# A fifth slot for queries and keys, its load placed behind the store of the maxima

## The chip, the cores and the metric

One core of one Trainium2 chip runs the whole program. The metric is the device time of one execution in microseconds (us). PE is the matrix engine (TensorE), DVE the vector engine, ACT the scalar engine, POOL GpSimd, SP the engine that only issues transfers here. "SPq" in a row is SP's queue of issues.

## The reference

A gated cross-attention block followed by a quantised feed-forward block, for x of 16 x 100 x 512 and a context of 16 x 361 x 512:

```python
Q = (layernorm(x) @ Wq) / sqrt(32)        # 16 heads of 32, in 4 groups
K, V = ctx @ Wk, ctx @ Wv                 # 4 heads of 32
scores = Q K^T + slope[h] * (key - query) # alibi, then the mask
x = x + tanh(g0) * (softmax(scores) V) @ Wo
q = round(layernorm(x), 8 bits per row);  Wg, Wu, Wd = ternary weights
h = rms_norm(silu(q Wg) * (q Wu)) * ln_w
x = x + tanh(g1) * round(h, 8 bits per row) @ Wd
```

A ternary weight is clip(round(w / mean|w|), -1, 1), so the mean over a whole weight must be known before the first one can be quantised.

## The kernel before

Everything is float32 in the attention. There are four stages.

1. **Queries** (to about 60 us). x is normalised, turned and projected in groups of four batches; each query tile is split into a high and a low float32r half and stored to `q_scratch` in DRAM.
2. **Context** (to about 148 us). For each of 16 batches `ct` is loaded, values go to `v_all`, keys (high and low) to `k_all`, which lies over the space that `w_q` takes later.
3. **Attention** (about 150 to 330 us). A batch needs its queries and keys in a *slot*: `qs[slot]` and `ks[slot]`, 103 rows, that `load_qk(b)` (line 397) gathers by six transfers on SP's queue: two from `q_scratch` (L402, 400 and 200 KB), three from `k_all` (L404, 181 KB each), and one of the mask row (L409). 1143 KB in all. Rows 96 to 102 hold constants (the alibi terms), written once for each slot. There are four slots; batch b uses slot b % 4. Slots 0 to 2 have their own space and get their constants from DVE; the fourth, `qs_late` and `ks_late`, lies over the context tiles, so that it exists only when the context stage is done; POOL copies its constants from slot 0 (`late_rows`, line 518).
4. **Feed-forward** (about 330 us to the end), in 13 tiles of rows.

In the attention PE works in *steps*, one per batch, of eight units each. In step b it computes the scores of batch b (`scores`, L1355, two matmuls per unit, whose row maxima DVE takes at L1021), and between them, by the table `BEHIND`, the transposed scores of older batches (`scores_t`, L1369), whose exponentials ACT takes at L725, and the products with values and ones (L1381, L1384). `scores_t(b - 1, 0)` is in unit 5 of step b; `scores_t(b - 2, 11)`, the last that reads slot (b - 2) % 4, stands in the same unit ahead of it.

The transposed scores need the maxima of their batch as two more rows (101 and 102) of the slot. DVE splits the maxima at the end of a step (`split_max`, L1028 and L1030), PE turns them in unit 1 of the next (L1392), ACT copies them to `nm_t`, and SP stores them into the slot with two transfers of 6.2 KB (`store_max`, L394). `scores_t(b, 0)` waits for both (`nm_in`). ACT waits for them too before it overwrites `nm_t` a step later.

SP issues strictly in this order, in `attention_step(b)` (line 424): `store_max(b - 1)`, then a wait until `scores_t(b - 2, 11)` is done, then `load_qk(b + 2)`. For b = 1 it is `store_max(0)`, a wait for the last key, the loads of batch 3, `store_max(1)`, a wait for POOL's constants, the mask row.

Meanwhile POOL quantises the feed-forward weights (`quantise`, line 532): 24 pieces of 128 x 1024, each a load of 512 KB on POOL's own queue and three operations (L535, L537, L542). The last writes `w_q`, over `k_all`, so piece n waits until the batches whose keys lie there are in their slots (L541). At the end of the attention PE waits for all 24. In step 9 ACT makes `wo_h` from `wo_f`, in step 10 DVE makes `wo_l` (L1079).

## Time and profile before

| | us |
|---|---|
| median of three runs | 527.29 |
| the three runs | 515.03, 527.29, 527.6 |
| the profiled execution | 515.34 |
| its span, first to last instruction | 513.5 |
| PE busy in the span | 466.4 (91%) |
| DVE / ACT / POOL busy | 368.2 / 320.5 / 230.5 |

The profiled execution stands with the lowest of the three runs; two of the three are about 12 us above it. All durations below are of the profiled one. Idle time in square brackets behind a row is that of the engine just before it, with what ended it.

### The profile page before, as it was taken

Reading aid. Unit: us, or ns where it says so; the run is one execution under the profiler, and the core shown is the slowest. Engines: PE = TensorE matmul, PEld = TensorE weight load, DVE = VectorE, ACT = ScalarE, POOL = GpSimd, SP = SyncE. Lnnn points to the kernel's source line nnn. Section 1 sums busy time; section 2 is a strip of 40 time slices with the busy share of each in tenths; the row PEclk is TensorE's granted clock in tenths of the full one; section 3 lists DMA queues with packets and bytes.
Section 4 is the critical chain, followed back from the end, with each engine's and each line's share of the span. In section 5 each row is a group of like instructions: output and inputs, shape, how many; then the busy total and the mean of one; then the engine's idle time right before and its main releaser. Section 6 shows DMA issues by size and latency. Waiting matters only on the chain.

```text
span 513.5 us, 8312 instructions
## 1 busy us (share of the span) xinstructions
PE 466.4 (91%) x2854; PEld 299.2 (58%) x2854; DVE 368.2 (72%) x674; ACT 320.5 (62%) x560; POOL 230.5 (45%) x250
## 2 busy tenths in 40 slices
PE   0699989999899999998899998988999999999966
PEld 0699989989875454554445554444444545555522
DVE  4778554448667887888978894377777778777762
ACT  0366626755656656666666666577777777777760
POOL 1100000000126787776362681057777777777630
PEclk9999998999999999999999999999999999999988
DMA  7879888899968889899676813014434333333323
GB/s 189 252 226 399 293 300 315 245 331 252 280 153 182 197 185 246 210 221 228 137 159 152 217 43 104 1 31 107 100 93 93 77 88 91 89 86 93 71 52 72
DMA packets 62834, 85.51 MB, mean 167 GB/s; under 512 B 37362, under 2 KB 48834, under 8 KB 61006
## 3 DMA queue, kind: packets, MB, share of 16 engines
q1 hardware_dynamic: 57614, 59.87, 47.3%
q0 software_dynamic: 3456, 12.58, 8.4%
q10 hardware_dynamic: 1728, 12.58, 7.0%
q8 instruction: 21, 0.34, 0.3%
q14 instruction: 15, 0.12, 0.1%
HBM read 57.94 MB, written 9.85 MB: 132 GB/s over the span
## 4 chain that ended last, share of the span: by engine, by line
PE 50%; DVE 15%; ACT 12%; DMA 12%; issue 6%; SPq 2%; ACTq 0%; POOL 0%; DVEq 0%; POOLq 0%
PE wide L1459 8%; DMA ct<-ctx_t 7%; PE bank L1288 6%; PE wide L1288 6%; PE bank L1381 5%; PE bank L1369 5%; PE bank L1329 5%; PE wide L1355 5%; PE bank L1469 5%; PE bank L1384 5%; DVE row_max L1021 3%; DMA qs<-nm_t 3%; ACT p_t L725 2%; DMA wq_f<-wq 2%; ACT act L837 2%
## 5 line engine op out<-in xcount | busy, mean ns | idle before, releaser
L1021 DVE TENSOR_REDUCE row_max<-wide 100x2 f32<-100x722 f32 x128 | 109.9, 903 | 21.0 <-PE wide L1355 20.0
L725 ACT ACTIVATE p_t<-bank 121x400 f32<-121x400 f32 x192 | 91.5, 506 | 52.5 <-PE bank L1369 49.3
L1459 PE MATMUL wide<-w_q,xq 128*128 128x512 bf16 x384 | 86.9, 380 | 2.7 <-DVE h L1139 2.4
L576 POOL TENSOR_TENSOR z<-h,lnw 128x512 f32<-128x512 f32 x48 | 61.1, 1275 | 15.2 <-DVE h L1139 14.6
L1459 PEld LDWEIGHTS wide<-w_q,xq 128*128 128x128 bf16 x384 | 35.5, 98 | 51.6 <-DVE h L1139 8.0
L1369 PE MATMUL bank<-qs,ks 103*121 103x400 f32 x144 | 52.0, 390 | 8.1 <-ACT p_t L725 5.5
L530 POOL DMA_DIRECT2D quant_in<-w_ffn x24 | 14.3, 597 | 98.0 <-PE bank L1329 91.5
L1329 PE MATMUL bank<-wv_f,ct 128*121 128x128 f32 x384 | 46.3, 278 | 4.0 <-DMA ct<-ctx_t 4.0
L968 DVE TENSOR_TENSOR ctl<-ct,cth 128x1445 fp32r<-128x1445 f32 x16 | 26.6, 1664 | 31.3 <-ACT cth L635 31.3
L1469 PE MATMUL bank<-w_q,yq 128*128 128x512 bf16 x192 | 46.5, 396 | 1.8 <-DMA yq<-y_int 1.7
L1329 PEld LDWEIGHTS bank<-wv_f,ct 128*121 128x121 f32 x384 | 45.4, 189 | 4.6 <-DMA ct<-ctx_t 4.6
L855 ACT ACTIVATE z<-z,small 128x1024 f32<-128x1024 f32 x24 | 29.7, 1237 | 29.5 <-DVE small L1173 29.5
L1369 PEld LDWEIGHTS bank<-qs,ks 103*121 103x121 f32 x144 | 25.3, 183 | 38.8 <-ACT p_t L725 15.5
L1355 PE MATMUL wide<-ks,qs 101*100 101x362 f32 x192 | 44.1, 333 | 2.1 <-ACT nm_t L635 1.5
L1139 DVE TENSOR_TENSOR h<-act,wide 128x512 f32<-128x512 f32 x50 | 34.2, 686 | 13.8 <-ACT act L837 13.5
L1381 PE MATMUL bank<-p_t,v_all 120*32 120x400 f32 (+1 forms) x384 | 42.9, 519 | 0.0
L1384 PE MATMUL bank<-p_t,ones_keys 120*32 120x400 f32 (+1 forms) x384 | 41.2, 501 | 0.0
L542 POOL TENSOR_SCALAR w_q<-quant_in 128x1024 bf16<-128x1024 f32 x24 | 27.5, 1147 | 25.2 <-DMA ks<-m_scratch 20.9
L837 ACT ACTIVATE act<-wide,small 128x512 f32<-128x512 f32 x50 | 33.7, 677 | 7.4 <-PE wide L1459 7.2
L535 POOL TENSOR_SCALAR quant_in<-quant_in,small 128x1024 f32<-128x1024 f32 x24 | 27.5, 1147 | 17.4 <-DMA quant_in<-w_ffn 16.6
L1469 PEld LDWEIGHTS bank<-w_q,yq 128*128 128x128 bf16 x192 | 19.0, 101 | 27.2 <-DMA yq<-y_int 3.9
L1355 PEld LDWEIGHTS wide<-ks,qs 101*100 101x100 f32 x192 | 30.5, 166 | 6.5 <-DVE row_max L1021 3.1
(160 smaller groups left out, 920.5 us busy)
## 6 DMA issues: line engine op xcount, KB each, us to landing
quant_in<-w_ffn POOLq DMA_DIRECT2D x24, 512.0 KB, 6.4
ct<-ctx_t SPq DMA_DIRECT2D x16, 722.0 KB, 10.6
abs_b<-w_ffn ACTq DMA_DIRECT2D x7, 1024.0 KB, 10.1
ks<-k_all SPq DMA_DIRECT2D x36, 181.0 KB
q_scratch<-qhl SPq DMA_DIRECT2D x16, 400.0 KB, 5.9
abs_a<-w_ffn ACTq DMA_DIRECT2D x5, 1024.0 KB, 6.6
qs<-q_scratch SPq DMA_DIRECT2D x12, 400.0 KB
xb<-x SPq DMA_DIRECT2D x12, 256.0 KB, 2.9
```

The source lines that it names most:

```text
L576: nc.gpsimd.tensor_tensor(z[par][0:rows, c], h[0:rows, c], lnw[0:rows, c], ALU.mult).then_inc(z_done, 1)
L725: nc.scalar.activation(p_t[:, j, :], bank[j % 2][0:KT, 0:HQ], ACT.Exp).then_inc(exp_done, 1)
L837: nc.scalar.activation(silu_g[j % 2][0:rows, :], wide[j % 2][0:rows, 0, :], ACT.Silu, scale=f_cg[par][0:rows]).then_inc(silu_done, 1)
L1021: nc.vector.tensor_reduce(row_max[b % 2][:, 2 * u:2 * u + 2], wide[u % 2][0:SQ, :, 0:SK], AX_X, ALU.max).then_inc(s_maxed, 1)
L1288: mm = nc.tensor.matmul(dst, a, b, start=(n == 0), stop=(n == last))
L1329: mm = nc.tensor.matmul(bank[2 + b % 2][0:KT, kt * P:(kt + 1) * P], tile[:, c * SK + k0:c * SK + k0 + KT], wv_f[:, c, :], start=(c == 0), ...
L1355: mm = nc.tensor.matmul(wide[u % 2][0:SQ, k, 0:SKP], qs[b % SLOTS][0:ROWS_S, g, h * SQ:(h + 1) * SQ], ks[b % SLOTS][0:ROWS_S, g, :], start ...
L1369: nc.tensor.matmul(bank[j % 2][0:KT, 0:HQ], ks[b % SLOTS][:, g, KT_AT[kt]:KT_AT[kt] + KT], qs[b % SLOTS][:, g, :], start=True, stop=True). ...
L1381: nc.tensor.matmul(bank[2][32 * g:32 * g + 32, 0:HQ], v_all[0:n, b, kt * P + DH * g:kt * P + DH * (g + 1)], p_t[0:n, kt * G + g, :], start ...
L1384: mm = nc.tensor.matmul(bank[3][32 * g:32 * g + 32, 0:HQ], ones_keys[0:n, :], p_t[0:n, kt * G + g, :], start=(kt == 0), stop=(kt == 2), ti ...
L1459: mm = nc.tensor.matmul(wide[j % 2][0:rows, m, :], xq[par][:, c, 0:rows], w_q[:, m * C + c, 512 * j:512 * j + 512], start=(c == 0), stop=( ...
L1469: mm = nc.tensor.matmul(bank[1][0:rows, :], yq[:, k, 0:rows], w_q[:, 2 * C + k // 4, (k % 4) * D:(k % 4 + 1) * D], start=(k == 0), stop=(k ...
```

## The change

There are five slots; batch b uses slot b % 5. The queries of both late slots and the keys of the fourth lie over the context tiles; the keys of the fifth lie at the end of the memory, where `log_sum` was, and `log_sum` moves over the context tiles. SP fills the constants of slots 3 and 4 by four transfers out of slot 0, and POOL's copies go. SP's order becomes `store_max(b - 1)`, a wait until `scores_t(b - 3, 11)` is done, `load_qk(b + 2)`. `wo_l` is written over `wo_f`. `oh` and `ol` move over the dead values of the first batches, and other feed-forward tiles move by some KB. Slot 0 is now read by the last batch, and the first product of the feed-forward (`h`, which lies over slot 0) waits for its transposed scores.

```diff
-SLOTS = 4
-LATE_SLOT = 3
+SLOTS = 5
+EARLY_SLOTS = 3
@@ memory
+    (qs3, ks3, qs4, log_sum), r_wo = over(r_c, ("qs3", [ROWS, G, HQ], F32R), ("ks3", [ROWS, G, SKP], F32R),
+                                          ("qs4", [ROWS, G, HQ], F32R), ("log_sum", [P, HQ], F32))
...
-    log_sum = new("log_sum", [P, HQ], F32)
+    ks.append(new("ks4", [ROWS, G, SKP], F32R))
...
-    (wo_f, wo_h, wo_l), e = over(
-        r_wo, ("wo_f", [P, HPG, D], F32), ("wo_h", [P, HPG, D], F32R), ("wo_l", [P, HPG, D], F32R))
+    (wo_l, wo_h), e = over(r_wo, ("wo_l", [P, HPG, D], F32R), ("wo_h", [P, HPG, D], F32R))
-    (oh, ol), e = over(r_wo, ("oh", [P, HPG, P], F32R), ("ol", [P, HPG, P], F32R))
+    (wo_f,), e = over(r_wo, ("wo_f", [P, HPG, D], F32))
@@ SP
+            def late_rows():
+
+                for slot in range(EARLY_SLOTS, SLOTS):
+                    for rows, src in ((qs[slot][96:101, :, :], qs[0][96:101, :, :]), (ks[slot][96:103, :, :], ks[0][96:103, :, :])):
+                        sp.dma_start(rows.bitcast(F32), src.bitcast(F32)).then_inc(rows_in, 16)
...
-                if b == LATE_SLOT:
+                if b == EARLY_SLOTS:
                     store_max(1)
-                    sp.wait_ge(late_set, 2)
+                    sp.wait_ge(rows_in, 64)
...
             def attention_step(b):
+                if b != 2:
+                    store_max(b - 1)
                 if b == 1:
-                    store_max(0)
                     sp.wait_ge(kl_ready, B)
-                    load_qk(LATE_SLOT)
-                elif b > 2:
-                    store_max(b - 1)
-                if 2 <= b < B - 2:
-                    sp.wait_ge(st_done, (b - 1) * UNITS)
+                    late_rows()
+                if b >= 3:
+                    sp.wait_ge(st_done, (b - 2) * UNITS)
+                if b < B - 2:
                     load_qk(b + 2)
@@ POOL
-            def late_rows():
-
-                pool.wait_ge(kl_ready, B)
-                pool.wait_ge(nm_split, 4)
-                nc.gpsimd.tensor_copy(qs_late[96:101, :, :], qs[0][96:101, :, :]).then_inc(late_set, 1)
-                nc.gpsimd.tensor_copy(ks_late[96:103, :, :], ks[0][96:103, :, :]).then_inc(late_set, 1)
-                pool.wait_ge(late_set, 2)
...
-            late_rows()
@@ DVE, by_up
-                if j == 0 and not (isinstance(t, int) and t == 0):
+                if j == 0 and isinstance(t, int) and t == 0:
+                    dve.wait_ge(st_done, B * UNITS)
+                elif j == 0:
                     dve.wait_ge(z_done, t * NJ)
```

## Rows read from the trace of the kernel before

**Rows 1.** The page, its first part: busy time of each engine in the span.

```profile
PE 466.4 (91%) x2854; PEld 299.2 (58%) x2854; DVE 368.2 (72%) x674; ACT 320.5 (62%) x560; POOL 230.5 (45%) x250
```

**Rows 2.** Windows, one attention step each: length, busy us, granted clock, DMA share, GB/s.

```profile
152.02:162.62 10.60, 10.54 (x79) 5.71 (x77) 7.77 (x11) 6.28 (x16) 9.52 (x10) 1.00 0.82 181
...
196.06:207.69 11.63, 10.37 (x78) 5.71 (x77) 9.06 (x14) 7.12 (x19) 8.22 (x9) 1.00 1.02 239
...
229.73:240.96 11.23, 10.96 (x78) 5.76 (x78) 9.94 (x14) 7.19 (x18) 8.70 (x9) 1.00 0.90 222
240.96:253.19 12.23, 10.44 (x78) 5.78 (x78) 10.85 (x14) 8.66 (x19) 4.87 (x5) 1.00 0.73 170
253.19:266.68 13.49, 12.17 (x79) 6.27 (x77) 10.87 (x15) 7.35 (x19) 8.60 (x8) 0.87 0.62 138
266.68:277.24 10.56, 10.30 (x78) 5.72 (x77) 8.79 (x14) 7.12 (x19) 3.80 (x4) 1.00 0.73 167
...
sum 158.06, PE 148.87 PEld 80.09 DVE 134.52 ACT 101.68 POOL 104.41; mean PE 10.63 PEld 5.72 DVE 9.61 ACT 7.26 POOL 7.46
```

**Rows 3.** Timeline of PE and PEld in the attention: start, us, instruction, idle before.

```profile
158.35 0.29 PEld L1369 LDWEIGHTS bank<-qs,ks 103*121 103x121 f32 x2 [0.65 <-DMA qs<-nm_t]
...
169.94 0.63 PE L1369 MATMUL bank<-qs,ks 103*121 103x400 f32 x2 [0.96 <-DMA qs<-nm_t]
...
203.42 0.63 PE L1369 MATMUL bank<-qs,ks 103*121 103x400 f32 x2 [1.00 <-DMA qs<-nm_t]
...
283.84 0.63 PE L1369 MATMUL bank<-qs,ks 103*121 103x400 f32 x2 [0.23 <-DMA qs<-nm_t]
...
310.87 0.39 PE L1288 MATMUL wide<-wo_h,oh 128*128 128x512 f32 x1
```

**Rows 4.** Timeline of SP's queue: when transfers are issued, and for how long.

```profile
149.07 1.13 SPq L402 DMA_DIRECT2D qs_late<-q_scratch  x2
150.24 1.95 SPq L404 DMA_DIRECT2D ks_late<-k_all  x3
152.88 1.21 SPq L394 DMA_DIRECT2D qs<-nm_t  x2
...
156.97 1.13 SPq L402 DMA_DIRECT2D qs<-q_scratch  x2
...
163.59 1.22 SPq L394 DMA_DIRECT2D qs<-nm_t  x2
167.53 1.42 SPq L402 DMA_DIRECT2D qs<-q_scratch  x2
...
271.60 1.13 SPq L402 DMA_DIRECT2D qs<-q_scratch  x2
...
278.21 1.22 SPq L394 DMA_DIRECT2D qs<-nm_t  x2
```

**Rows 5.** The tile `nm_t`: time from issue to landing of its 24 stores into early slots.

```profile
DMA to landing us min/median/max: 1.7/3.6/10.9
```

**Rows 6.** Timeline of POOL: the copies, and a weight piece that waited, the first `ol`.

```profile
151.23 1.52 POOL L522 CAST qs_late<-qs 5x1600 fp32r<-5x1600 f32 x1 [13.79 <-DVE nm_q L1030]
...
154.22 1.12 POOL L535 TENSOR_SCALAR quant_in<-quant_in,small 128x1024 f32<-128x1024 f32 x1
...
283.56 1.05 POOL L542 TENSOR_SCALAR w_q<-quant_in 128x1024 bf16<-128x1024 f32 x1 [8.01 <-DMA ks<-m_scratch]
...
305.10 2.39 POOL L565 TENSOR_TENSOR ol<-o_t,oh 128x512 fp32r<-128x512 f32 x1
```

**Rows 7.** Timeline of DVE: the split of the maxima slow and quick, and `wo_l`.

```profile
239.19 1.50 DVE L1028 TENSOR_SCALAR nm_q<-row_max 100x16 fp32r<-100x16 f32 x1
...
251.75 0.18 DVE L1028 TENSOR_SCALAR nm_q<-row_max 100x16 fp32r<-100x16 f32 x1
...
252.05 2.28 DVE L1079 TENSOR_TENSOR wo_l<-wo_f,wo_h 128x2048 fp32r<-128x2048 f32 x1
```

**Rows 8.** Windows: the five microseconds in which the granted clock fell.

```profile
255.00:260.00 5.00, 4.79 (x25) 2.32 (x26) 4.02 (x6) 1.55 (x5) 2.53 (x3) 0.66 0.17 35
```

More of the change, by code:

```diff
@@ L138, in flamingo_block @@
     r_a = place[0]
-    (qs_late, ks_late), r_wo = over(r_c, ("qs_late", [ROWS, G, HQ], F32R), ("ks_late", [ROWS, G, SKP], F32R))
-    qs = [qs_late if i == LATE_SLOT else new(f"qs{i}", [ROWS, G, HQ], F32R) for i in range(SLOTS)]
-    ks = [ks_late if i == LATE_SLOT else new(f"ks{i}", [ROWS, G, SKP], F32R) for i in range(SLOTS)]
+    (qs3, ks3, qs4, log_sum), r_wo = over(r_c, ("qs3", [ROWS, G, HQ], F32R), ("ks3", [ROWS, G, SKP], F32R),
+                                          ("qs4", [ROWS, G, HQ], F32R), ("log_sum", [P, HQ], F32))
+    qs = [new(f"qs{i}", [ROWS, G, HQ], F32R) for i in range(EARLY_SLOTS)] + [qs3, qs4]
+    ks = [new(f"ks{i}", [ROWS, G, SKP], F32R) for i in range(EARLY_SLOTS)] + [ks3]
     r_p = place[0]
@@ L178, in flamingo_block @@
     assert e <= r_a
-    (wo_f, wo_h, wo_l), e = over(
-        r_wo, ("wo_f", [P, HPG, D], F32), ("wo_h", [P, HPG, D], F32R), ("wo_l", [P, HPG, D], F32R))
+    (wo_l, wo_h), e = over(r_wo, ("wo_l", [P, HPG, D], F32R), ("wo_h", [P, HPG, D], F32R))
     assert e <= r_i
-    (oh, ol), e = over(r_wo, ("oh", [P, HPG, P], F32R), ("ol", [P, HPG, P], F32R))
+    (wo_f,), e = over(r_wo, ("wo_f", [P, HPG, D], F32))
     (lnw,), e = over(r_i, ("lnw", [P, F], F32))
     assert e <= r_a
-    (xb0, xb1, x1_0, x1_1, xd, xq_f, xq0, xq1, x_int, act0, act1, ident_b), e = over(
-        r_v, ("xb0", [P, D], F32), ("xb1", [P, D], F32), ("x1_0", [P, D], F32), ("x1_1", [P, D], F32),
-        ("xd", [P, D], F32), ("xq_f", [P, D], F32), ("xq0", [P, C, P], BF16), ("xq1", [P, C, P], BF16), ("x_int", [P, D], BF16), ("act0", [P, 512], F32),
-        ("act1", [P, 512], F32), ("ident_b", [P, P], BF16))
+    (oh, ol, xb0, xb1, x1_0, x1_1, xd, xq_f, xq0, ident_b, act0, act1, xq1, x_int), e = over(
+        r_v, ("oh", [P, HPG, P], F32R), ("ol", [P, HPG, P], F32R), ("xb0", [P, D], F32), ("xb1", [P, D], F32),
+        ("x1_0", [P, D], F32), ("x1_1", [P, D], F32), ("xd", [P, D], F32), ("xq_f", [P, D], F32), ("xq0", [P, C, P], BF16),
+        ("ident_b", [P, P], BF16), ("act0", [P, 512], F32), ("act1", [P, 512], F32), ("xq1", [P, C, P], BF16), ("x_int", [P, D], BF16))
     assert e <= r_c
@@ L252, in flamingo_block @@
         alibi_set = sem("alibi_set")
-        late_set = sem("late_set")
+        rows_in = sem("rows_in")
         mask_set = sem("mask_set")
```

## The prediction

> **What bounds the kernel now.** I read the page first, then the chain that ended last, then PE's timeline through the attention, then SP's queue beside it. PE is busy 466.4 of 513.5 us [rows 1], so time can be won only where PE stands still. The change touches nothing ahead of 149 us and no work behind about 333 us, so the question is what PE loses in the 14 attention steps between.
>
> A table of windows cut at the turn of the maxima gives the steps: 158.06 us for 14. The two shortest are 10.60 and 10.56 us, with PE busy 10.54 and 10.30 [rows 2]: that is a step in which nothing is late. At 10.56 each, 14 steps would take 147.8, so 10.2 us is lost, and it goes to three causes.
> - Three steps hold a stop of PE at `scores_t(b, 0)` that a store of maxima ended: 0.96, 1.00 and 0.23 us, 2.2 in all [rows 3]. The step around the second is 11.63 long, 1.0 more than a free one [rows 2].
> - The steps in which `wo_h` and `wo_l` are made: 12.23 and 13.49 [rows 2], 4.6 us of loss. `wo_l` holds DVE for 2.28 us while maxima wait [rows 7], and behind it the granted clock is 0.66 over five microseconds, in part the lower of its two levels (1.2 instead of 2.4 GHz), after a step in which PE was busy only 10.44 of 12.23 us [rows 2, 8]. That alone is 5 x 0.34 = 1.7 us.
> - The rest, 10.2 - 2.2 - 4.6 = 3.4 us, lies in steps such as the one of 11.23 [rows 2], near whose end the split of the maxima took 1.50 us where it takes 0.18 otherwise [rows 7]; POOL was busy 8.70 us of it [rows 2].
>
> Why is a store late? SP's queue shows it. `store_max` is issued in unit 1 (163.59), and PE wants it in unit 5. The load of 1143 KB ahead of it was issued at 156.97 [rows 4]. In a step with such a stop the transfers' share is 1.02 [rows 2]: the engines are full, with POOL's weight loads among them. Late in the stage a wait of POOL dates the end of a load: the load begun at 271.60 landed just ahead of 283.56 (11.7 to 12.0 us), and POOL's piece had waited 8.01 us for it [rows 4, 6]. The store issued at 278.21 stood behind it and PE got it at 283.84 [rows 3, 4]. In the 11 steps without a stop on a store it was in time. So a store lands with the load ahead of it, and is late when that is over 5.4 us after its own issue (168.98 less 163.59, [rows 3, 4]). Its shortest landing is 1.7 us, the median 3.6 [rows 5].
>
> The Trainium skill, page "DMA: Bandwidth & Descriptors", section "Queues, rings and completion order", says that descriptors of one engine are taken in ring order and that a semaphore's increment lands only after every earlier write from that engine. By that rule a load put behind the store costs the store nothing; by the opposite case (both share the bandwidth) the store would take about its median and still be in time. The trace agrees with the rule: the store landed with the load ahead of it. The sum below does not need it.
>
> **The change, part by part.**
>
> *Load behind the store, steady state.* The load waits for a batch that finished a step ago, so it is issued 1.2 us after the store's issue began: 164.8 instead of 167.53, or 268.9 instead of 271.60 [rows 4], 2.7 us earlier. With 12.0 us to land, 268.9 gives 280.9, 2.7 us after the next store's issue at 278.21; PE needs the store 5.4 us after it. The stops of 1.00 and 0.23 us go: -1.2. Bounds: 0, if weight loads take the room that is freed; and -2.4, if the median landing hides small delays elsewhere; I take -1.2, the rows themselves. The fifth slot means that no load waits for PE and that no score waits for a load: none did before.
>
> *Late rows on SP.* This is the part with a price. From 149.07 SP issues four more transfers. An issue is 0.57 to 0.65 us (1.13 for two, 1.95 for three) [rows 4], so 4 x 0.6 = 2.4 us. Then come the five of the load, 3.1 us, so `store_max(1)` is issued at 154.6 and not at 152.88: 1.7 later, for 0.7 us of waiting for ACT was there to absorb it. PE wants it at 158.35; there the wait before was 0.65 us, its usual gap [rows 3]. The store needs between 3.6 us (median, [rows 5]) and 6.3 (163.59 to 169.9, [rows 3, 4]) from issue: it lands at 158.2 to 160.9, a stop of 0 to 2.5 us. Nearest is a store behind one uncontended load (that load began at 149 with an empty queue), so I take the lower middle, +1.0. The copies move 5 x 6400 and 7 x 5792 bytes per slot, 145 KB in all: at 181 GB/s [rows 2] 0.8 us of transfer, inside those bounds. If fewer transfer engines share them it is still under the 2.4 us of issue. `rows_in` is awaited after ten later issues, so it costs nothing; what is queued behind that wait is the mask row and the next load, whose reader starts at 161.5.
>
> *The second store.* The load of batch 4 now follows the mask row (one more issue of 0.6 behind the store's two) at about 156.4 instead of 156.97, only 0.5 us earlier, and behind a first load that began 2.4 us later. So `store_max(2)` still stands in a full queue. But PE comes to it 1.0 later by the part above. The stop of 0.96 us goes to about 0.1: -0.9 (bounds: 0 and -0.96).
>
> *POOL without copies.* POOL starts weight pieces at 151.4 and not at 154.22 [rows 6], 2.9 us sooner. Later pieces wait for loads that come 2.7 us sooner. The last operation then ends near 302 instead of 305; behind it stands `ol` (305.10) [rows 6], which is done at 307.5 and which PE takes only at 310.87, without a wait [rows 3]. Worth 0, hidden behind attention on PE; without that cover at most 2.9.
>
> *Contention.* The moved pieces meet other DVE operations. The 3.4 us of the third cause may vanish or double: 0, bounds -3.4 and +3.4. The Trainium skill, page "SBUF — State Buffer", section "Who interferes with whom", says that GpSimd and certain VectorE operations take one port pair as an exclusive lock, the later one blocking for a whole instruction. The slow splits beside a busy POOL agree. It gives no sign for this change.
>
> *`wo_l` in place.* Same instruction, same size: 0. The transfer of `wo_f` comes earlier with the load ahead of it, and ACT reads it steps later: 0. The clock's fall stays as long as `wo_l` blocks DVE: 0, bounds -1.7 (it does not fall) and +1.7 (it falls once more).
>
> *The added wait on DVE.* `by_up(0, 0)` needs the first silu, which ACT runs only after the last four exponentials of batch 15, and these follow the last transposed scores. The wait is over before it is reached: 0; behind it would stand all of DVE's feed-forward work. SP's waits in steps 14 to 16 are for batches done a step before: 0. Moved tiles change no instruction's size: 0.
>
> Sum: +1.0 - 0.9 - 1.2 = -1.1. Profiled execution 515.34, so **514.2 us**. Against the median shown, 527.29, that is 13 less, but 12 of these are the distance of the profiled execution from the median and not the change; a median from the upper cluster would be 527.3 - 1.1 = 526.2.
>
> **The rivals.**
> 1. *The start costs more than the stops give (slower).* `store_max(1)` lands at 160.9, and, because load 3, load 4 and the copies are now back to back in a full queue, `store_max(2)` is late by another 1.7 us. +2.5 + 1.7 - 1.2 = +3.0: 518.3. It decides from a landing of `store_max(1)` after about 159.8 us. For it: a share of 1.02 in the step at 196. Against it: step 2 has 0.82, so there was room. Chance 0.2.
> 2. *Late stores are the 12 us.* The upper runs are 12.0 to 12.3 us above the profiled one, and 14 steps with a stop of 0.87 us would be just that; the two long stops seen are 0.96 and 1.00. If transfers are a little slower there, the change takes all of it: about 514 in every run, 2.4% under the median. For it: the fit, and stores that land close to the need. Against: two such tight clusters look like no matter of transfer rates. Chance 0.14.
> 3. *Contention falls as well.* Stops and slow splits all go: 515.34 - 2.2 - 3.4 = 509.7. Chance 0.12.
> 4. *No effect.* Weight loads fill the room that the earlier load leaves, and the stops stay: 515 to 516. Chance 0.1.
>
> **How the numbers follow.** The forecast has the remaining 0.44. All but the second rival lie within 2% of before if like runs are compared (about what a measurement of this kernel can tell from no change); 2% is 10.3 us, more than all that the steps lose, so faster has 0.14 of the second rival and 0.02 of luck. Slower by 2% needs 0.7 us in every step: a contention that locks on, 0.06. The range runs from 509.5 (third rival) to 527 (the forecast in the upper cluster); the forecast's own is 511 to 517.
>
> **What would show it.** Right: no stop on `nm_t` at PE from step 4 on; loads on SP's queue 1.2 us behind the store's issue; POOL's waits for slots shorter by 2 to 3 us; a stop of about 1 us at `scores_t(1, 0)`; FFN unchanged from its first product on. Wrong: stops of PE by stores in later steps; a `store_max(1)` landing past 160; more than five slow splits at L1028; another fall of the clock.

## The result, and the profile after

| | before | after |
|---|---|---|
| median, us | 521.69 (12 executions) | 526.92 (12 executions) |
| lowest to highest | 515.03 to 529.72 | 524.45 to 531.14, and one of 927.18 |
| profiled execution | 515.34 | 525.0 |
| its span | 513.5 | 523.1 |
| mean granted clock in it | 0.987 | 0.972 |

The changed kernel takes 1.0131 times as long (95% interval 1.01 to 1.0162): 1.3% slower, where -1.1 us was forecast. This ratio leaves out the slow executions of each kernel (more than 1.5% above its fastest), which the medians in the table include; the medians alone are 1.0% apart. The execution of 927.18 us left no trace; its cause is open, and the median doesn't hang on it. The two profiled executions are 9.6 us of span apart, more than the 5.2 us between the medians, since the profiled one of before was among its quickest. Eight of the 12 executions of before lie between 519.7 and 523.9, where the first three had none: the prediction's "upper cluster" was an accident of three draws.

The page after, busy time of each engine and the line of the granted clock in 40 slices ([rows 1] before):

```profile
PE 469.3 (90%) x2854; PEld 301.4 (58%) x2854; DVE 365.7 (70%) x674; ACT 320.2 (61%) x560; POOL 225.8 (43%) x248
...
PEclk9999998999996999999789999999999999999998
```

The same number of matmuls is 2.9 us longer on PE, so only part of the 9.6 us is standing still; the clock line has a 6 and a 7 in the attention. Windows after, cut at the turn of the maxima as in [rows 2] (length, busy us of PE, PEld, DVE, ACT, POOL, granted clock, DMA share, GB/s):

```profile
151.28:171.42 20.14, 12.99 (x78) 6.70 (x77) 7.33 (x11) 6.26 (x16) 12.05 (x14) 0.75 0.94 189
...
182.53:193.09 10.56, 10.30 (x78) 5.71 (x77) 8.87 (x14) 7.12 (x19) 8.49 (x9) 1.00 0.94 207
...
246.59:261.83 15.24, 13.19 (x79) 7.16 (x77) 9.43 (x14) 9.12 (x20) 5.62 (x7) 0.78 0.56 127
261.83:275.76 13.93, 12.37 (x78) 6.10 (x77) 11.86 (x15) 7.23 (x19) 8.35 (x7) 0.88 0.70 162
275.76:286.32 10.56, 10.30 (x79) 5.70 (x77) 8.86 (x14) 7.11 (x19) 2.81 (x4) 1.00 0.69 163
```

Where the 9.6 us are:

| part | before | after | difference |
|---|---|---|---|
| up to the first turn | 152.02 | 151.28 | -0.7 |
| step 2 | 10.60 | 20.14 | +9.5 |
| the steps with `wo_h` and `wo_l` | 12.23 + 13.49 | 15.24 + 13.93 | +3.4 |
| the other eleven steps | 121.74 | 118.07 | -3.7 |
| from the last turn to the end | 203.42 | 204.44 | +1.0 |

One step lost as much as the whole kernel did; the other differences cancel out. PE's timeline after, the stops of its matmuls in the attention that are over 0.5 us ([rows 3] before):

```profile
164.76 1.02 PE L1367 MATMUL bank<-qs,ks 103*121 103x400 f32 x2 [7.10 <-DMA qs<-nm_t]
...
221.19 0.62 PE L1367 MATMUL bank<-qs,ks 103*121 103x400 f32 x2 [0.61 <-DMA qs<-nm_t]
...
248.88 0.69 PE L1367 MATMUL bank<-qs,ks 103*121 103x400 f32 x1 [2.05 <-ACT p_t L721]
...
264.03 0.57 PE L1353 MATMUL wide<-ks,qs 101*100 101x362 f32 x2 [1.24 <-DVE row_max L1017]
```

At `scores_t(1, 0)` PE stands 7.10 us for `store_max(1)`. The chain that ended last goes through that transfer for 9.38 us:

```profile
155.34 9.38 DMA qs<-nm_t
164.72 0.04 issue
164.76 1.02 PE bank L1367 x2
```

SP's queue after ([rows 4] before). The four copies are L401, load 3 begins at 151.37, the store is at 154.66, the load of batch 4 behind it at 156.66:

```profile
148.32 0.76 SPq L401 DMA_DIRECT2D qs<-qs  x1
149.12 0.75 SPq L401 DMA_DIRECT2D ks<-ks  x1
149.92 0.68 SPq L401 DMA_DIRECT2D qs<-qs  x1
150.64 0.69 SPq L401 DMA_DIRECT2D ks<-ks  x1
151.37 1.27 SPq L408 DMA_DIRECT2D qs<-q_scratch  x2
152.69 1.92 SPq L410 DMA_DIRECT2D ks<-k_all  x3
154.66 1.28 SPq L394 DMA_DIRECT2D qs<-nm_t  x2
155.98 0.64 SPq L415 DMA_DIRECT2D ks<-m_scratch  x1
156.66 1.14 SPq L408 DMA_DIRECT2D qs<-q_scratch  x2
...
172.39 1.22 SPq L394 DMA_DIRECT2D qs<-nm_t  x2
173.65 1.88 SPq L408 DMA_DIRECT2D qs<-q_scratch  x2
```

And POOL, which now has no copies to make. It frees its first weight slot, and issues the next load of 512 KB at 154.40, 3.0 us behind load 3; before, the same load left at 157.89, 8.8 us behind load 3:

```profile
150.73 1.12 POOL L532 TENSOR_SCALAR quant_in<-quant_in,small 128x1024 f32<-128x1024 f32 x1 [14.04 <-DVE small L1008]
...
154.40 0.59 POOL L527 DMA_DIRECT2D quant_in<-w_ffn  x1 [0.30 <-POOL w_q L539]
```

Stretches of one microsecond after (same columns as the windows): in the stop nothing runs on any engine, the transfers are full, and the granted clock is 0.50, that is 1.2 GHz; it is back from 170 on.

```profile
150.00:151.00 1.00, 1.00 (x6) 0.78 (x7) 0.93 (x8) 0.86 (x3) 0.27 (x1) 1.00 0.39 47
...
160.00:161.00 1.00, 0.00 (x0) 0.00 (x0) 0.00 (x0) 0.00 (x0) 0.00 (x0) 0.50 1.02 234
...
169.00:170.00 1.00, 1.00 (x8) 0.00 (x0) 0.00 (x0) 0.00 (x0) 0.34 (x1) 0.53 0.29 59
170.00:171.00 1.00, 1.00 (x9) 0.93 (x6) 0.15 (x1) 0.81 (x3) 0.88 (x1) 1.00 0.82 191
```

From 164.8 until just before 170 PE works at half speed, and its busy time in step 2 is 12.99 us where it was 10.54: 2.4 us more for the same work. 7.1 + 2.4 = 9.5 is the growth of step 2.

### The profile page after: what moved, and what is told of

Its sections match the earlier page's. It is cut to its first block, busy times and chain, and to the rows that moved or that the text cites. A ratio compares the mean times of both kernels' runs of the same rounds, so it can differ in the third digit from the quotient of the medians.

```text
span 523.1 us, 8317 instructions
## 1 busy us (share of the span) xinstructions
PE 469.3 (90%) x2854; PEld 301.4 (58%) x2854; DVE 365.7 (70%) x674; ACT 320.2 (61%) x560; POOL 225.8 (43%) x248
## 4 chain that ended last, share of the span: by engine, by line
PE 61%; DMA 12%; ACT 10%; DVE 10%; issue 3%; SPq 2%; POOL 0%; ACTq 0%; POOLq 0%; DVEq 0%
PE wide L1457 12%; PE bank L1286 8%; DMA ct<-ctx_t 7%; PE bank L1379 6%; PE bank L1367 6%; PE wide L1286 6%; PE bank L1467 6%; PE bank L1382 5%; PE wide L1353 5%; PE bank L1327 5%; ACT p_t L721 3%; DMA qs<-nm_t 3%; DMA wq_f<-wq 1%; DVE row_max L1017 1%; ACT sum_kept L739 1%
## 5 line engine op out<-in xcount | busy, mean ns | idle before, releaser
L1367 PE MATMUL bank<-qs,ks 103*121 103x400 f32 x192 | 70.2, 397 | 16.1 <-ACT p_t L721 8.0
L1367 PEld LDWEIGHTS bank<-qs,ks 103*121 103x121 f32 x192 | 34.2, 186 | 59.5 <-issue 22.6
L1353 PE MATMUL wide<-ks,qs 101*100 101x362 f32 x256 | 59.9, 338 | 3.0 <-DVE row_max L1017 1.5
L1467 PE MATMUL bank<-w_q,yq 128*128 128x512 bf16 x192 | 45.2, 388 | 2.6 <-DMA yq<-y_int 2.6
L1353 PEld LDWEIGHTS wide<-ks,qs 101*100 101x100 f32 x256 | 42.3, 172 | 7.6 <-DVE row_max L1017 3.3
L1379 PE MATMUL bank<-p_t,v_all 120*32 120x400 f32 (+1 forms) x384 | 44.2, 534 | 0.0
L1382 PE MATMUL bank<-p_t,ones_keys 120*32 120x400 f32 (+1 forms) x384 | 43.1, 522 | 0.0
L532 POOL TENSOR_SCALAR quant_in<-quant_in,small 128x1024 f32<-128x1024 f32 x24 | 29.4, 1223 | 31.7 <-DMA quant_in<-w_ffn 17.1
L539 POOL TENSOR_SCALAR w_q<-quant_in 128x1024 bf16<-128x1024 f32 x24 | 27.5, 1146 | 32.6 <-DMA ks<-m_scratch 31.2
## 6 DMA issues: line engine op xcount, KB each, us to landing
quant_in<-w_ffn POOLq DMA_DIRECT2D x24, 512.0 KB, 7.0
abs_b<-w_ffn ACTq DMA_DIRECT2D x7, 1024.0 KB, 10.4
```

The costliest lines, as they stand in the source:

```text
L1353: mm = nc.tensor.matmul(wide[u % 2][0:SQ, k, 0:SKP], qs[b % SLOTS][0:ROWS_S, g, h * SQ:(h + 1) * SQ], ks[b % SLOTS][0:ROWS_S, g, :], start ...
L1367: nc.tensor.matmul(bank[j % 2][0:KT, 0:HQ], ks[b % SLOTS][:, g, KT_AT[kt]:KT_AT[kt] + KT], qs[b % SLOTS][:, g, :], start=True, stop=True). ...
L1379: nc.tensor.matmul(bank[2][32 * g:32 * g + 32, 0:HQ], v_all[0:n, b, kt * P + DH * g:kt * P + DH * (g + 1)], p_t[0:n, kt * G + g, :], start ...
L1382: mm = nc.tensor.matmul(bank[3][32 * g:32 * g + 32, 0:HQ], ones_keys[0:n, :], p_t[0:n, kt * G + g, :], start=(kt == 0), stop=(kt == 2), ti ...
L1467: mm = nc.tensor.matmul(bank[1][0:rows, :], yq[:, k, 0:rows], w_q[:, 2 * C + k // 4, (k % 4) * D:(k % 4 + 1) * D], start=(k == 0), stop=(k ...
```

## The experiments

The theory: what counts is when load 3 starts, and what runs beside it until `store_max(1)` has landed. The runs e3 to e7, e10 and e12 to e14 are one execution each, read for the stop at `scores_t(1, 0)` and not for their time; e3 and e10, which turned out to have the same order of transfers, differ by 0.3 us in it. The rivals: the copies' transfer itself blocks the engines; the four issues alone do it; the fifth slot's order (load behind store) is bad in every step.

**e1_pool_rows.** POOL fills the constants of both late slots, as before it did for one; all the rest is the changed kernel.

```diff
-                    late_rows()                     # SP
-                    sp.wait_ge(rows_in, 64)
+                    sp.wait_ge(rows_in, 4)
...
+            def late_rows():                        # POOL, behind load_quant(1)
+                pool.wait_ge(kl_ready, B)
+                pool.wait_ge(nm_split, 4)
+                for slot in range(EARLY_SLOTS, SLOTS):
+                    nc.gpsimd.tensor_copy(qs[slot][96:101, :, :], qs[0][96:101, :, :]).then_inc(rows_in, 1)
+                    nc.gpsimd.tensor_copy(ks[slot][96:103, :, :], ks[0][96:103, :, :]).then_inc(rows_in, 1)
+                pool.wait_ge(rows_in, 4)
```

> The kernel after with one part undone: POOL, not SP, copies the constants of both late slots (four copies of about 1.5 us, so the weight pieces start near 157 instead of 151). Theory A (the four copies on SP's queue hold up the load and the store of the maxima behind them): the stop of 7.1 us at scores_t(1, 0) goes to under 1 us, the step around it is near 10.6 instead of 20.1, and the time is 8 to 12 us under the kernel after. Theory B (POOL's weight load, 2.9 us earlier, takes the room): this run removes that too, so the same fall; only the second run tells A from B. Theory C (the load of batch 4 directly behind the store holds it up): the stop stays, 5 us or more.

Measured: 517.8 us (median of 10 executions) beside 521.53 for the kernel before, ratio 0.9956 (0.9899 to 1.0013). No stop at `scores_t(1, 0)`: counted from load 3's issue the store landed after 8.9 us, and PE is ready after 9.3 (below), so there would be none even without the fall of the granted clock that this trace has from 151 to 159. The landing of its two stores, and POOL's first weight piece behind four copies:

```profile
DMA to landing us min/median/max: 3.7/3.7/3.8
```

```profile
155.59 1.39 POOL L549 CAST ks<-ks 7x1448 fp32r<-7x1448 f32 x1
157.09 1.11 POOL L531 TENSOR_SCALAR quant_in<-quant_in,small 128x1024 f32<-128x1024 f32 x1
```

So the loss is in the way the late slots are filled, and not in five slots or in the load behind the store: with that alone put right, 1.3% slower becomes 0.4% faster, though that interval still touches 1. It does not say which part of it was dear, since this edit takes the copies off SP and also holds POOL's weight load back (its load leaves at 160.76).

**e2_rows_behind.** The same four transfers, issued behind `store_max(1)`.

```diff
-                    late_rows()
 ...
                     store_max(1)
+                    late_rows()
                     sp.wait_ge(rows_in, 64)
```

> The kernel after with SP's four copies issued behind store_max(1) instead of ahead of the load of batch 3. The weight pieces keep their early start. Theory A: the stop goes to under 1 us, 8 to 12 us under the kernel after. Theory B: the stop stays at 3 us or more, for the weight load issued near 154 is still there. Theory C: the stop shrinks only by the 2 us that the load of batch 4 is held back.

Measured: 523.3 beside 521.53, ratio 1.008 (0.9996 to 1.0163). The stop is gone from `scores_t(1, 0)`, but 4.3 of its 7.1 us went into new ones:

```profile
167.80 0.76 PE L1353 MATMUL wide<-ks,qs 101*100 101x362 f32 x2 [2.52 <-DMA ks<-m_scratch]
...
178.06 0.62 PE L1367 MATMUL bank<-qs,ks 103*121 103x400 f32 x2 [1.76 <-DMA qs<-nm_t]
```

SP had stood at its wait for the copies from 160.6 to 165.84 before it could issue the mask row of batch 3, which the first score of that batch needs. The copies are issued in 3.0 us wherever they stand; behind load 3, with POOL's load (158.60) beside them, they had landed only at 165.8; the wait on them, priced at nothing in the prediction, has a price here.

**e3_quant_later.** POOL holds its first weight piece, and with it the loads that follow (in the changed kernel at 154.40 and 158.71), until `store_max(1)` has landed.

```diff
             load_quant(1)
+            pool.wait_ge(nm_in, 64)
             pool.wait_ge(w_scale_set, 1)
```

> The kernel after with POOL's first weight piece held until the store of the second maxima has landed; the copies stay ahead of the load on SP's queue. Theory A: the stop stays near 7 us, less at most the 2.5 us that 512 KB take. Theory B: the stop falls to 2 us or less.

```profile
162.37 1.02 PE L1368 MATMUL bank<-qs,ks 103*121 103x400 f32 x2 [4.68 <-DMA qs<-nm_t]
```

Measured: 523.02, span 521.1. The stop is 4.68 and not 7.10: 2.4 us of it are POOL's loads, the one 3.0 us behind load 3 and the next one 7.3 us behind it. No run separates the two.

**e4_load4_later.** The load of batch 4 waits until the transposed scores of batch 0 are done.

```diff
-                if b >= 3:
-                    sp.wait_ge(st_done, (b - 2) * UNITS)
+                if b >= 2:
+                    sp.wait_ge(st_done, max(b - 2, 1) * UNITS)
```

> The kernel after with the load of batch 4 held until the transposed scores of batch 0 are done (157, as before). Theory A: the stop stays within 1 us of 7.1. Theory C: it falls to 3 us or less.

Measured: 521.62, stop 3.78 us, but load 4 left 4.05 us behind the store (160.38), still ahead of its landing, and PE came to its step later after a fall of the clock from 152 to 159. It is read beside e13 and e12 below.

**e5_await_rows.** SP waits until the copies have landed before it issues load 3, to time them alone.

```diff
                         sp.dma_start(rows.bitcast(F32), src.bitcast(F32)).then_inc(rows_in, 16)
+                sp.wait_ge(rows_in, 64)
```

> The kernel after with SP waiting for its four copies to land before it issues the load of batch 3, so that the copies run alone and SP's next issue dates their landing. If the copies are cheap, as the prediction had it (0.8 us of transfer, about 2 us to land), SP goes on near 153.5, 2 us after the last of the four issues. If they hold their transfer engines for long, as the second experiment hints (SP stood 5 us on them), SP goes on at 155 or later. The stop at scores_t(1, 0) is then the landing of the load behind them: 6 us or more in either case.

Measured: 528.64, stop 8.37. SP's queue, and two stretches of one microsecond in which almost only the copies run:

```profile
151.93 0.76 SPq L401 DMA_DIRECT2D qs<-qs  x1
...
154.24 0.69 SPq L401 DMA_DIRECT2D ks<-ks  x1
157.77 1.13 SPq L409 DMA_DIRECT2D qs<-q_scratch  x2
```

```profile
154.00:155.00 1.00, 1.00 (x7) 0.69 (x5) 0.96 (x6) 0.86 (x3) 0.66 (x1) 1.00 0.37 47
155.00:156.00 1.00, 1.00 (x6) 0.61 (x4) 1.00 (x2) 0.99 (x4) 0.92 (x2) 1.00 0.36 43
```

The 145 KB take 5.8 us from the first issue until SP goes on (151.93 to 157.77), 3.0 us of it the four issues, at 47 GB/s or less and a DMA share of 0.37 or less. The prediction had 0.8 us from 181 GB/s.

**e6_rows_pool_queue.** The same four transfers from POOL's queue; SP issues none of them.

```diff
-                    late_rows()                     # SP
...
+                        nc.gpsimd.dma_start(rows.bitcast(F32), src.bitcast(F32)).then_inc(rows_in, 16)   # POOL, x4
```

> The kernel after with the same four copies issued on POOL's queue instead of SP's. If SP's own order of issue and its ring are what delays the store, the stop at scores_t(1, 0) goes to 1 us or less and the time is near that of the run with POOL's own copies. If the copies' hold on the transfer engines is it, whatever queue they come from, a stop of 2 us or more stays.

```profile
163.05 0.63 PE L1374 MATMUL bank<-qs,ks 103*121 103x400 f32 x2 [3.10 <-DMA qs<-nm_t]
...
177.60 0.63 PE L1374 MATMUL bank<-qs,ks 103*121 103x400 f32 x2 [2.30 <-DMA qs<-nm_t]
```

Measured: 526.28. Load 3 starts first on SP (150.60) and the store still comes 3.10 us late. The store's two issues took 1.85 and 0.86 us here instead of 0.59 each; why is open. As transfers beside load 3, the copies are not free on another queue either.

**e7_issue_alone.** POOL makes the copies, and SP issues four transfers of 128 bytes in their place, within DRAM, that nobody reads; the computation is whole.

```diff
-                for slot in range(EARLY_SLOTS, SLOTS): ...
...
+                for i in range(4):
+                    sp.dma_start(idle_scratch[i:i + 1], alibi_q[0:1, 0, 0:32]).then_inc(idle_in, 16)
```

> The kernel with POOL's copies, and four transfers of 128 bytes on SP's queue where the kernel after has its copies: issue time alone, without their bytes. If 2.4 us of issue are the harm, the stop at scores_t(1, 0) is 2 us or more; if it is the copies' bytes, the stop is 1 us or less, though SP issues store_max(1) as late as in the kernel after.

Measured: 532.82, stop 4.77, landing 8.7. Load 3 was issued at 156.56, and the window from 156 to 160 shows only 29 GB/s, so the run does not price issuing alone. It is inconclusive for what it was made for.

**e10_both_held.** The edits of e3 and e4 together.

```diff
+            pool.wait_ge(nm_in, 64)                                        # POOL, as in e3
+                    sp.wait_ge(st_done, max(b - 2, 1) * UNITS)             # SP, as in e4
```

> The kernel after, its four copies on SP's queue ahead of the load of batch 3 as they are, but with both neighbours of the store held: POOL's first weight piece until the second maxima have landed, and the load of batch 4 until the transposed scores of batch 0 are done. If the long stop is made of three things that share the transfer engines (the copies ahead, the weight load beside, the load of batch 4 behind), the stop at scores_t(1, 0) is now 0.5 to 2.5 us, as the prediction sized the copies alone, and the store lands within 5.5 us of its issue. If the copies alone make it, the stop stays above 4 us.

Measured: 523.56, stop 4.40, landing 6.4. SP's wait was over when it was reached and load 4 left at 158.74, 2.0 us behind the store as in the changed kernel: this is e3 once more, and repeats its number (4.68) to 0.3 us; it does not test the pair.

**e13_load4_truly_held.** Load 4 waits for the landing of `store_max(1)` itself; POOL's load is left where the change put it.

```diff
+                if b == 2:
+                    sp.wait_ge(nm_in, 64)
                 if b >= 3:
```

> The kernel after with only the load of batch 4 held until the second maxima have landed; POOL's weight load stays early. If the load behind has a share, the stop falls from 7.1 us to 4 to 5.5 us; if not, it stays within 0.5 us of 7.1.

```profile
163.90 1.02 PE L1369 MATMUL bank<-qs,ks 103*121 103x400 f32 x2 [4.68 <-DMA qs<-nm_t]
```

Measured: 522.85, span 520.9. The load *behind* the store costs it 2.4 us, as much as POOL's do.

**e12_both_truly_held.** The edits of e3 and e13 together: nothing but the copies ahead runs beside load 3.

```diff
+            pool.wait_ge(nm_in, 64)                                        # POOL, as in e3
+                if b == 2:
+                    sp.wait_ge(nm_in, 64)                                  # SP, as in e13
```

> The kernel after with POOL's first weight piece and SP's load of batch 4 both held until the second maxima have landed, so that nothing runs beside the copies, the load of batch 3 and the store. If the load behind the store has a share in its lateness, the stop at scores_t(1, 0) falls from 4.4 us to 1 to 3 us (the copies put the store 1.7 us late and hold some transfer engines). If only the copies count, it stays at 4 us or more.

```profile
162.57 0.63 PE L1370 MATMUL bank<-qs,ks 103*121 103x400 f32 x2 [2.88 <-DMA qs<-nm_t]
```

Measured: 519.2, span 517.4. Both neighbours gone take 4.2 us off the stop, and 2.88 remain.

**e14_half_the_rows.** As e12, but only slot 3's two copies stand ahead of load 3; slot 4's follow the landing of the store.

```diff
-                    late_rows()
+                    late_rows(3)
+                if b == 2:
+                    sp.wait_ge(nm_in, 64)
+                    late_rows(4)
+                    sp.wait_ge(rows_in, 64)
```

> As the run with both held, and only the copies for slot 3 stand ahead of the load of batch 3; those for slot 4 follow behind the store. Two issues less (1.4 us) and half the bytes: the stop falls by 1.4 us if issue time alone counts, by more if the copies also hold transfer engines, and may be gone. The load of batch 4 comes late by this and may stop PE at the next store.

```profile
163.95 0.62 PE L1372 MATMUL bank<-qs,ks 103*121 103x400 f32 x2 [0.30 <-DMA qs<-nm_t]
...
180.74 1.02 PE L1372 MATMUL bank<-qs,ks 103*121 103x400 f32 x2 [6.16 <-DMA qs<-nm_t]
```

Measured: 529.2. The first stop is down to 0.30. But load 4, held until 167.66, stands right ahead of `store_max(2)` and makes that one 6.16 us late: the same mechanism one step on, with another load.

**The runs side by side.** All times but the first two columns are counted from load 3's first issue. "Landed" is the start of PE behind the stop; for the two without a stop (before, e1) and for e2 it is the second store's issue plus the longest landing.

| kernel | SP's first issue | load 3 | POOL's load | load 4 | landed | stop |
|---|---|---|---|---|---|---|
| before | 149.07 | 149.07 | 8.8 | 7.9 | 9.0 | 0 |
| e1 | 149.15 | 149.15 | 11.6 | 8.5 | 8.9 | 0 |
| e2 | 152.51 | 152.51 | 6.1 | 14.0 | 9.4 | 0 |
| e12 | 150.36 | 153.41 | 12.9 | 9.1 | 9.2 | 2.88 |
| e5 | 151.93 | 157.77 | 0.2 | 5.5 | 11.9 | 8.37 |
| e6 | 150.60 | 150.60 | 6.1 | 9.8 | 12.5 | 3.10 |
| e14 | 153.26 | 154.85 | 12.8 | 12.8 | 9.1 | 0.30 |
| e7 | 154.08 | 156.56 | 9.1 | 6.1 | 12.7 | 4.77 |
| e3 | 148.35 | 151.40 | 14.7 | 5.4 | 11.0 | 4.68 |
| e10 | 150.29 | 153.34 | 14.4 | 5.4 | 10.7 | 4.40 |
| e13 | 149.87 | 152.92 | 3.0 | 11.0 | 11.0 | 4.68 |
| e4 | 149.92 | 152.97 | 3.0 | 7.4 | 12.6 | 3.78 |
| after | 148.32 | 151.37 | 3.0 | 5.3 | 13.4 | 7.10 |

"POOL's load" is the first of POOL's behind load 3; where that is at 3.0, a second follows at 7.3 to 7.4 (after, e13, e4), and in e5 at 4.6.

PE is ready for `scores_t(1, 0)` 9.3 us behind SP's first issue (before 158.35 - 149.07; after 164.76 - 7.10 - 148.32 = 9.34; the same in e3, e5, e6, e10, e12 and e13). So the stop is (load 3's delay) + (landed) - 9.3:
- e12: 3.05 + 9.16 - 9.33 = 2.88. The delay by four issues, and nothing else. Copies that stand whole ahead of the load cost it no time beyond their issue: landed is 9.2 with them and 9.0 without.
- e3 and e13: 3.05 + 11.0 - 9.3 = 4.7. Either neighbour alone (load 4, or POOL's loads) adds 1.8.
- after: 3.05 + 13.4 - 9.3 = 7.1. Both together add 4.2. The run e4 fits between: with load 4 at 7.4 instead of 5.3 it is 3.5, and its stop is shorter than that because PE itself came 2.6 later.
- e5: 5.84 + 11.9 - 9.3 = 8.4. Load 3 waits for the copies' whole length instead of their issue. With the copies landed, its neighbours add 2.7 and not 4.2; POOL's loads stand elsewhere here, so whether copies still in flight make the neighbours dearer stays open.
- e6: 0 + 12.5 - 9.3 = 3.1. Here the copies are the neighbour.
- e14: two copies ahead delay load 3 by 1.59; 1.59 + 9.10 = 10.7, and PE was ready 10.4 behind the first issue, not 9.3, after a clock of 0.50 between 156 and 159. So of the 2.6 us by which this stop is shorter than e12's, 1.5 are issues saved and 1.1 are PE's own delay.

The table decides between the rivals: the copies' long transfer (5.8 us alone) was a wrong suspect while it stood ahead on the same queue, though beside load 3 (e6) it counts; the issues are 3.05 of 7.1, less the 0.2 by which PE's need comes behind the landing of an undisturbed load, and what runs beside load 3 is 4.2: load 4 and POOL's loads. In e2, where POOL's load starts 6.1 behind, it is at most 0.4, no more than the spread.

**e9_before_split_wo.** A control for the two `wo` steps: in the kernel before, `wo_h` and `wo_l` are made in quarters, one a step, instead of one block of 1.92 us on ACT and one of 2.28 on DVE.

```diff
-                if b == 9:
+                if 9 <= b <= 12:
-                    copy_high(wo_h[:, :, :], wo_f[:, :, :])
+                    copy_high(wo_h[:, b - 9, :], wo_f[:, b - 9, :])
...
-                if b == 10:
-                    dve.wait_ge(wo_high, 1)
...
+                if 10 <= b <= 13:
+                    dve.wait_ge(wo_high, b - 9)
...
```

> The kernel before with wo_h and wo_l made in quarters, one per step, and nothing else: control for the part of the gain that has nothing to do with slots. If the two blocks let the clock fall, the time falls by 3 to 5 us against before (ratio 0.990 to 0.995) and the granted clock of its runs lies above that of before.

Measured: 518.82 (12 executions) beside 522.42, ratio 0.9947 (0.9894 to 1.0001): the gain is of the size expected, and its interval just touches 1. The granted clock of the trace does not fall in the attention any more.

**e8_pool_rows_split_wo** and **e11_split_wo_again** are one kernel: e1 with the quarters of e9.

> The kernel with POOL's copies, and wo_h and wo_l made in four quarters each, one per step, instead of one block of 1.92 us on ACT and one of 2.28 us on DVE. If the stops of PE behind these two blocks let the clock fall, the two steps around them (13.8 and 13.7 us in the run with POOL's copies) go to 11 to 11.5 each, the granted clock there stays at 1.00, and the time falls by 3 to 6 us, to about 513. If the clock falls for another reason, the falls move elsewhere and the gain is 2 us or less.

> The same kernel as the run with POOL's copies and wo in quarters, again beside the control: what the five slots with POOL's copies add to it. If the order of loads and stores is worth the stops it removed (1 to 2 us) the ratio is 0.003 to 0.006 under that of the control; if not, the two are alike.

Measured: 515.61 beside 521.68, ratio 0.989 (0.9827 to 0.9953), and again 514.35 (12 executions) beside 522.42, ratio 0.9894 (0.9842 to 0.9946). Windows of e8, the first two steps with quarters, where after has 15.24 and 13.93:

```profile
245.11:256.57 11.46, 10.53 (x79) 5.70 (x77) 10.88 (x15) 7.64 (x20) 4.63 (x5) 1.00 0.72 179
256.57:267.65 11.08, 10.31 (x79) 5.77 (x77) 10.11 (x15) 7.65 (x20) 6.73 (x6) 1.00 0.69 155
```

The page of e11 (14 of its matmul records are missing, so its PE time is not compared); no slice of the attention is under 9:

```profile
PE 462.5 (91%) x2840; PEld 299.7 (59%) x2854; DVE 369.9 (72%) x677; ACT 319.7 (63%) x563; POOL 229.8 (45%) x252
...
PEclk9999998999999999999999999999999999999989
```

This version is 1.1% under before, clear of noise, and before is 1.3% under the changed kernel. Half of the 1.1% comes with the quarters alone (e9). The other half would be the slots' order with POOL's copies: the ratio is 0.0053 under e9's, as expected, but the two intervals overlap, so this half is not shown by itself.

## Why the prediction was wrong, step by step

**Late rows on SP: +1.0 forecast, 7.1 measured. This is the step that failed**, in three terms.
- The issue of the store: forecast 1.7 us later (154.6), measured 154.66 instead of 152.88, right. But counted from SP's first issue it is 2.5 later, for SP and PE both came 0.7 earlier. Four copies are 3.05 us of issue (0.68 to 0.76 each), not 2.4.
- The landing: forecast 3.6 to 6.3 us from the store's first issue, measured 10.1 (154.66 to 164.72); with both neighbours held it is 5.9 (e12, 156.68 to 162.57), inside the forecast but at its upper end. The prediction had just said that a store lands with the load ahead of it. It should have followed its own rule and dated the store by load 3: PE took it 9.3 us behind load 3's start [rows 3, 4], so some 151.4 + 9.3 = 160.7 with nothing new beside it, where PE was ready at 157.66: a stop of 3.0 us, and e12 shows 2.88. It took a median over all stores instead [rows 5], most of which have an old load ahead of them.
- The neighbours: forecast nothing, measured 4.2. No other load started beside load 3 for 7.9 us before, and for 3.0 after.

**POOL without copies: 0 forecast.** "2.9 us sooner, worth 0, hidden behind attention" looked only at the end of POOL's work. That this costs nothing was right, though not for the forecast end of 302: the last `w_q` piece ends at 308.8, `ol` at 310.1, and PE takes it at 319.70 without a wait. But POOL's copies were also what kept its next loads of 512 KB from load 3. Their earlier start costs 2.4 of the 7.1 us (e3). Nor did the pieces gain by it: POOL's waits for slots grew from 23.5 us (20.9 and 2.6) to 31.2, where they should have become shorter. The waits of before and of after:

```profile
POOL w_q L542 <- DMA ks<-m_scratch: 20.9, 3, 8.3
...
POOL w_q L542 <- DMA ks_late<-m_scratch: 2.6, 1, 2.6
```

```profile
POOL w_q L539 <- DMA ks<-m_scratch: 31.2, 7, 8.2
```

**Load behind the store: no cost forecast, 2.4 measured at the start** (e13), nothing seen in most later steps. A difference that fits, though no run varied it in steady state, is the age of the load ahead: 3.3 us when `store_max(1)` is issued at the start. In steady state it is 9.3 (a step of 10.56 less the 1.26 by which the load follows a store), and the load is nearly done. The prediction cited the page "DMA: Bandwidth & Descriptors", section "Queues, rings and completion order", of the Trainium skill for ring order and drew from it that a load behind costs nothing. That went beyond the page: it says in which order one engine takes descriptors and what an increment waits for, not that a later transfer leaves the engines' rate to the earlier one, and it says that the increment waits for earlier writes "across its queues". The second half fits what e3 shows, POOL's loads from another queue counting too; the 11.0 us of e3 against the 9.2 of e12, which differ by load 4 alone, decide against the reading made of the first. How the engines divide between the two loads no run shows.

**Steady state: right in kind, and the sum was better than forecast in part by luck.** The eleven ordinary steps are 3.7 us shorter. All three stops of before lie in them, and -2.1 was forecast for these (-0.9 and -1.2); stops on stores fell from 2.2 us to 0.6, so -1.6. From step 4 on there is one stop on `nm_t` at a matmul of PE, 0.61 us, against 1.00 and 0.23. Loads leave 1.26 us behind the store's issue (173.65 behind 172.39), as forecast. The rest, some 2.1 us, goes with the third cause of loss: the split of the maxima, which took 1.50 us or more in five steps before, is never above 0.47 after, though POOL is nearly as busy. That is the mechanism of rival 3, which had a chance of 0.12. It looks like a matter of phase: in all five of before's, POOL began the first operation of a weight piece 0.33 to 0.35 us behind the split's start, and both ended together, as here beside the split at 239.19 [rows 7]:

```profile
239.53 1.13 POOL L535 TENSOR_SCALAR quant_in<-quant_in,small 128x1024 f32<-128x1024 f32 x1
```

Nothing in the change aims at this phase, and changed kernels have slow splits again (six of 0.99 to 1.41 us in e1, 1.07 and 1.51 in e12), so these 2.1 us are best taken as luck.

**The second store: -0.9 forecast, and it came,** but for a poor reason: `store_max(2)` had no stop since PE came to it almost 10 us later.

**The clock: forecast 0, with +1.7 for one more fall. The bound was too small.** The first extra fall is that of the stop (2.4 us). The second stands behind `wo_h`: a stop of 2.05 us, where before had 1.79 and no fall, and then 0.50 until 255. The two `wo` steps together lost 3.4 more than before's. The first is caused by the change. The second is not shown to be: in the 13 traces with `wo` in whole blocks the clock fell behind `wo_l` in all, and behind `wo_h` in 10, but not in before and not in e4 and e13, which have the change; in the three with quarters (e9, e8 and e11) it fell behind neither. So the blocks bring the falls, and before's trace was one of the few with a single fall. The traces are 9.6 apart and the medians 5.2; 9.5 at the start less 3.7 in the ordinary steps is 5.8, and the other 3.4 + 1.0 - 0.7 are differences that a second pair of traces need not show.

**Rival 1 had the mechanism, and its price was wrong.** A start that costs more than the stops give, decided by a landing of `store_max(1)` after 159.8: it landed at 164.72. It was priced at +3.0, since its landing was the same bound of 6.3 us. Its further delay of `store_max(2)` did not come. What spoke against it in the prediction, "step 2 has 0.82, so there was room", was an average: before, while load 3 was in flight, the transfers were full, and the room came behind it.

```profile
155.00:156.00 1.00, 1.00 (x11) 0.52 (x4) 0.00 (x0) 0.06 (x1) 0.92 (x2) 1.00 1.05 166
...
157.00:158.00 1.00, 1.00 (x16) 0.29 (x12) 1.00 (x2) 0.69 (x2) 0.70 (x2) 1.00 0.00 0
```

**Rival 2 falls.** In the 19 executions of before beside e1 the time goes with the mean granted clock: 512.63 us at 0.989, 517.92 at 0.980, 526.44 at 0.967, 530.62 at 0.965. A late store could lower the clock too, so this alone does not clear it. But e1 and e11, in which most stores are in time, still spread from 512.0 to 521.91 and from 509.67 to 521.67, and the changed kernel did not go to 514.

**Right at their value of nothing:** `wo_l` in place (2.29 us against 2.28), the added waits of DVE and SP, the feed-forward stage: its first product is 20.3 us behind the last turn (20.2 before), and it ends 184.1 us later (183.2). Those 0.9 us lie where only the places of tiles were changed; no run explains them.

## What to carry over

When something is put ahead of a load, date everything behind it by that load's start plus its whole length with its new neighbours, not by the median landing of small transfers. An engine that loses work in a change starts its next transfer sooner: ask what that transfer will meet, even where the engine has time to spare. A mean share of busy transfers over a step does not say that there is room in it: look at the stretch in which the new transfer will run. A stop of PE of a few microseconds costs more than its length when the granted clock falls behind it (7.1 + 2.4 here), and work of 2 us in one piece on ACT or DVE that makes PE wait is better cut into pieces (0.5% in e9).

## What the hardware did that was not expected

- **Copies of a few partitions inside SBUF are slow.** Four transfers with 5 and 7 rows, 145 KB together, took 5.8 us alone (e5), 3.0 of it issuing, with a DMA share of 0.37 or less at 47 GB/s or less. The Trainium skill, page "DMA: Bandwidth & Descriptors", section "Why a DMA increments its semaphore by 16 and not by 1", says that a transfer is spread over the largest number of engines up to 16 that divides its slowest dimension, here 5 or 7 of 16. A share of 5/16 to 7/16 (0.31 to 0.44) fits the 0.34 to 0.39 measured in the stretches that the copies fill (e5 and after); no run changed the shape to test it. On POOL the same rows take 1.52 [rows 6] and 1.39 us (e1) a slot.
- **Neighbours of a load cost more together than one by one:** 1.8 us for load 4 (e3) or for POOL's two loads (e13), 4.2 for all of them (after against e12). With the copies out of the way and POOL's loads earlier they cost 2.7 (e5), so the surplus is not a constant.
- **A load of 1143 KB behind four transfers of 128 bytes within DRAM** got going late (e7: 29 GB/s in the window from 156 to 160, issued at 156.56) and landed 12.7 us behind its issue, with load 4 beside it, instead of 9.0. That the small transfers held it is an inference; why is open.
- **The granted clock falls behind some short stops, and their length alone does not decide it.** In the changed kernel it went to 0.50 behind stops of 7.10 us (until 170), 2.05 (until 255) and 1.24 (266 to 268). In the attention of all 16 traces it fell behind each of the 13 stops of 2.30 us or more, behind 10 of the 13 stops of 1.77 to 2.06 us that `wo_h` brings, and behind all 13 of 1.00 to 1.24 us that `wo_l` brings one step later; it did not fall behind single stops of 1.30 to 1.76 us elsewhere (e2, e5, e8, e11, e14). In e1, e4, e7, e8 and e14 it was also at 0.50 near the start of the attention (for example from 152 to 159 in e4), where no stop is over 0.5 us.
